# First attention of a four-stage kernel: each head's query and key rows stacked as high and low parts, 48 to a head, through a DRAM scratch

## The reference

```
def _L0_attn_ref(x, Wq, Wk, Wv, Wo):
    NH = 16
    B, T, D = x.shape
    hd = D // NH
    q = (x @ Wq.T).reshape(B, T, NH, hd).transpose(0, 2, 1, 3)
    k = (x @ Wk.T).reshape(B, T, NH, hd).transpose(0, 2, 1, 3)
    v = (x @ Wv.T).reshape(B, T, NH, hd).transpose(0, 2, 1, 3)
    att = jnp.einsum('bhtd,bhsd->bhts', q, k) / jnp.sqrt(jnp.asarray(hd, x.dtype))
    att = att + jnp.triu(jnp.full((T, T), neg, dtype=att.dtype), k=1)
    w = jax.nn.softmax(att, axis=-1)
    z = jnp.einsum('bhts,bhsd->bhtd', w, v)
    return z.transpose(0, 2, 1, 3).reshape(B, T, D) @ Wo.T
```

## Time and profile before

| | |
|---|---|
| runs | 968.06 us median (967.4, 968.06, 969.87) |
| profiled execution | 971.69 us, of which the trace spans 969.5 us |
| PE busy | 837.5 us of the span, 86% |
| DVE, ACT, POOL busy | 668.5, 389.0, 394.3 us |
| mean granted clock of TensorE | 0.916 |
| rounds 0 to 6 of the first attention | 38.74 to 239.71 us |
| round 7 and what follows it | from 239.71 us |

### The profile page before, as it was taken

The page is one execution under the profiler, slowest core; times in us unless marked ns, Lnnn a source line. Parts: engine busy times, 40 slices in busy tenths (PEclk is TensorE's granted clock), DMA queues, the critical chain, the costliest instruction groups (busy, mean ns, idle before and its releaser), DMA issues. The chain is left out here.

```text
span 969.5 us, 18748 instructions
## 1 busy us (share of the span) xinstructions
PE 837.5 (86%) x6718; PEld 702.1 (72%) x6718; DVE 668.5 (69%) x1501; ACT 389.0 (40%) x764; POOL 394.3 (41%) x548
## 2 busy tenths in 40 slices
PE   5889999998778968778898869899989999999994
PEld 4667777677557857667776758688878888788883
DVE  6657767677358644898565566577898775867876
ACT  2244444444542353333343344355556554222220
POOL 3123323333522237777776561756664221100001
PEclk9899999999889988999999976677898988999998
DMA  7002112200000057999940352211110000000001
GB/s 260 2 2 99 56 45 99 100 12 13 13 11 0 23 154 224 292 285 305 301 139 2 88 162 65 71 39 48 33 54 27 0 1 1 1 0 22 23 1 43
DMA packets 51385, 75.57 MB, mean 78 GB/s; under 512 B 9810, under 2 KB 43869, under 8 KB 51176
## 3 DMA queue, kind: packets, MB, share of 16 engines
q1 hardware_dynamic: 27624, 43.01, 13.6%
q0 software_dynamic: 9856, 18.92, 7.0%
q10 hardware_dynamic: 13824, 12.59, 3.8%
HBM read 70.27 MB, written 31.46 MB: 105 GB/s over the span
## 5 line engine op out<-in xcount | busy, mean ns | idle before, releaser
L537 POOL DMA_INDIRECT work<-xnd,rows_at x128 | 132.8, 1037 | 49.6 <-issue 42.9
L454 POOL TENSOR_SCALAR veps<-mv 128x2 f32<-128x2 f32 (+1 forms) x63 | 15.5, 246 | 284.3 <-DVE mv L1574 284.1
L463 POOL TENSOR_SCALAR_AFFINE_SELECT work<-work 128x256 f32<-128x256 f32 x128 | 53.5, 442 | 118.9 <-ACT work L659 118.8
L2013 DVE TENSOR_TENSOR work<-work,S 64x256 f32<-64x256 f32 x128 | 54.2, 424 | 55.6 <-ACT work L811 53.7
L972 PE MATMUL ZO<-parts 128*128 128x256 f32 x224 | 71.1, 318 | 16.1 <-DVE parts L1613 6.0
L972 PE MATMUL S<-xr,parts 128*128 128x512 f32 x192 | 83.0, 432 | 0.8 <-issue 0.8
L791 ACT ACTIVATE work<-S 128x512 f32<-128x512 f32 x64 | 38.2, 597 | 101.0 <-PE S L1311 97.0
L974 PE MATMUL S<-xr,parts 128*128 128x512 f32 x192 | 76.9, 401 | 0.0
L973 PE MATMUL S<-xr,parts 128*128 128x512 f32 x192 | 76.8, 400 | 0.0
L659 ACT ACTIVATE work<-S 128x768 f32<-128x768 f32 x64 | 51.7, 811 | 53.9 <-PE S L1046 53.9
L1311 PE MATMUL S<-ident,work 128*128 128x128 f32 x256 | 43.3, 293 | 28.8 <-DMA work<-xnd,rows_at 27.9
(11 more groups left out here) (331 smaller groups left out, 2337.0 us busy)
## 6 DMA issues: line engine op xcount, KB each, us to landing
yd<-work ACTq DMA_DIRECT2D x128, 128.0 KB
raw<-in_experts SPq DMA_DIRECT2D x74, 192.0 KB
work<-in_experts SPq DMA_DIRECT2D x36, 192.0 KB
lg_all<-in_experts SPq DMA_DIRECT2D x18, 192.0 KB
xnd<-attn_w SPq DMA_DIRECT2D x8, 256.0 KB, 2.1
shd<-work SPq DMA_DIRECT2D x8, 256.0 KB, 2.4
work<-xnd,rows_at POOLq DMA_INDIRECT x128
raw<-in_ffn SPq DMA_DIRECT2D x2, 1024.0 KB, 6.3
```

The lines of the kernel that those rows point to most:

```text
L463: last = pool.affine_select(out=diagonal, in_=diagonal, compare_op=ALU.is_ge, fill=0.0, base=0, pattern=[[0, 2], [1, P]], channel_multipli ...
L537: pool.indirect_dma_start(xg[:, i % RING, b, :], None, xnd[:], bass.IndirectOffsetOnAxis(ap=rows_at[:, k:k + 1], axis=0), bounds_check=NT ...
L2013: last = dve.tensor_tensor(hx[64 * half:64 * half + 64, i % 2, :], sgx[64:128, i % 2, :], S[2 + i % 2][64:128, 0:256], ALU.mult)
```

## The change

The weights are no longer doubled: a sequence has two calls of `project_qk` (c is 0 or 1) in place of four, each with the queries of eight heads and their keys. ACT writes their high parts in one copy of 512 columns (`qk_hi`), DVE their low parts in one subtraction (`qk_lo`). SP then stores high, high and low to planes of a DRAM tensor `qkd` (three transfers of 256 KB) and loads from it four blocks of 48 rows (192 KB each), in which a head's rows are query high, low, high (`QROWS`) and key high, high, low (`KROWS`), at partitions 0 to 47 for r=0 and 64 to 111 for r=1. The host orders the weights' columns for that (`units`).

One matmul over 48 rows now does what two passes did, so the turned scores are two passes: scores of 48 rows, and the selector by the row maxima, still 32 rows (`shift`). Plain scores use all 48 rows too, and unit u uses its own heads. Around it: `input_transposes` moves from u5 to u2, `project_qk(i+2, 0)` from u6 to u3, `project_qk(i+2, 1)` from u7 to u6, `router_logits` from u3 to u7; the first round (i = -1) has `project_v(0)`, `input_transposes(1)` and `project_qk(1, 0)` ahead of its units. SP stages the first three halves of sequences ahead of the later weights' loads, the fourth behind them, and the 2 MB copies to `yd` move to the last rounds. Two semaphores are merged with others.

```
-        wq_p, wk_p, wv_p, wo_p, xn_p, z_p = (in_parts(n) for n in (512, 512, D, D, T, T))
+        wq_p, wk_p, wv_p, xn_p = (in_parts(n) for n in (D, D, D, T))
+        qk_hi = parts[:, words[0]:words[0] + 2 * T]
...
+            def score_rows(b, c):
+                n = 2 * b + c
...
+                sp.wait_ge(s["a_q"], n + 1)
+                sp.dma_start(planes(0, 3), stage(qk_hi)).then_inc(s["q_st"], 16)
+                sp.dma_start(planes(2, 2), stage(qk_hi)).then_inc(s["q_st"], 16)
+                sp.wait_ge(s["a_k"], n + 1)
+                sp.dma_start(planes(1, 4), stage(qk_lo)).then_inc(s["q_st"], 16)
+                sp.wait_ge(s["q_st"], 48 * (n + 1))
+                if n:
+                    sp.wait_ge(s["q_in"], 64 * n)
+                if b >= 2:
+                    sp.wait_ge(s["a_st"], 8 * (b - 2) + 4 * c + 4)
+                for r in range(2):
+                    for first, rows in ((0, QROWS), (3, KROWS)):
+                        sp.dma_start(rows[64 * r:64 * r + 48, b % 2, 4 * c:4 * c + 4, :].bitcast(F32)
+                                     .rearrange("p u t -> p (u t)"),
+                                     qkd[c, first:first + 3, 64 * r:64 * r + 64, :]
+                                     .rearrange("k (e u) t -> k e (u t)", u=4)).then_inc(s["q_in"], 16)
...
+            for b, c in ((0, 0), (0, 1), (1, 0)):
+                score_rows(b, c)
+            later_weights()
+            score_rows(1, 1)
+            for i in range(NB + 1):
+                if i + 2 < NB:
+                    score_rows(i + 2, 0)
+                if i:
+                    normed_rows(i - 1)
+                if i + 2 < NB:
+                    score_rows(i + 2, 1)
+                if i > NB - 3:
+                    result_rows(i - NB + 2)
+            result_rows(3)
...
-            def query_copies(b, g):
-                act.wait_ge(s["a_qk"], 4 * b + g + 1)
-                act.activation(qh0, O[:, 0:T], ACT.Copy)
-                act.activation(kh0[:, b % 2, g, :], O[:, T:2 * T], ACT.Copy).then_inc(s["a_q"], 1)
+            def score_highs(b, c):
+                n = 2 * b + c
+                act.wait_ge(s["a_qk"], n + 1)
+                if n:
+                    act.wait_ge(s["q_st"], 48 * n)
+                act.activation(qk_hi, O, ACT.Copy).then_inc(s["a_q"], 1)
...
+                    if u % 4 == 0:
+                        pe.wait_ge(s["q_in"], 64 * (2 * nb + u // 4 + 1))
...
-                    for k in range(3):
+                    for shift in range(2):
                         for half in range(2):
                             for r in range(2):
-                                last = turned(r, half, k)
+                                last = turned(r, half, shift)
...
-            def key_copies(b, g):
-                dve.wait_ge(s["a_q"], 4 * b + g + 1)
-                dve.scalar_tensor_tensor(qm0[:, b % 2, g, :], qh0, negm[:, 0:1], O[:, 0:T], ALU.mult, ALU.add)
-                dve.tensor_tensor(kl0[:, b % 2, g, :], O[:, T:2 * T], kh0[:, b % 2, g, :], ALU.subtract
-                                  ).then_inc(s["a_k"], 1)
+            def score_lows(b, c):
+                dve.wait_ge(s["a_q"], 2 * b + c + 1)
+                dve.tensor_tensor(qk_lo, O, qk_hi, ALU.subtract).then_inc(s["a_k"], 1)
```

More of the change, by code:

```diff
@@ L389, in _, with planes, stage @@
[L389 to L393, removed]
+            def score_rows(b, c):
+                n = 2 * b + c
+                flat = qkd[c].rearrange("k p t -> p k t")
+                def planes(first, step):
+                    return flat[:, first:first + step + 1:step, :]
+                def stage(part):
+                    return part.bitcast(F32).rearrange("p (k t) -> p k t", k=2)
+                sp.wait_ge(s["a_q"], n + 1)
[14 more added lines that the diff above has]
+                                     .rearrange("k (e u) t -> k e (u t)", u=4)).then_inc(s["q_in"], 16)
@@ L982, in _, with project_qk @@
             M = (SS[:, 0:1024], TT)
-            def project_qk(b, g):
-                if g == 0:
+            def project_qk(b, c):
+                if c == 0:
                     pe.wait_ge(s["a_xtl"], b + 1)
                 else:
[L988 to L993, removed]
+                    pe.wait_ge(s["a_q"], 2 * b + 1)
+                    pe.wait_ge(s["a_k"], 2 * b + 1)
                 for w, o in ((wq_p, 0), (wk_p, T)):
-                    for c in range(KC):
-                        last = three(O[:, o:o + T], lambda k: w[:, k, c, g * P:(g + 1) * P],
-                                     lambda k: xn_p[:, k, c, :], c == 0, c == KC - 1)
+                    for k in range(KC):
+                        last = three(O[:, o:o + T], lambda part: w[:, part, k, c * P:(c + 1) * P],
+                                     lambda part: xn_p[:, part, k, :], k == 0, k == KC - 1)
                 last.then_inc(s["a_qk"], 1)
             def project_v(b):
-                pe.wait_ge(s["a_q"], 4 * b + 2)
-                pe.wait_ge(s["a_k"], 4 * b + 2)
+                if b >= 3:
+                    pe.wait_ge(s["a_xall"], b - 1)
+                else:
+                    pe.wait_ge(s["a_q"], 2 * b + 2)
+                    pe.wait_ge(s["a_k"], 2 * b + 2)
                 if b == 0:
                     pe.wait_ge(s["a_wl"], 3)
-                if b >= 3:
-                    pe.wait_ge(s["a_xall"], b - 1)
                 for t in range(2):
@@ L1129, in attention @@
                     maxima_rows(i)
+                if i == -1:
+                    project_v(0)
+                    input_transposes(1)
+                    project_qk(1, 0)
                 for u in range(8):
@@ L1149, in attention @@
                     if 0 <= i + 2 < NB and u == 6:
-                        project_qk(i + 2, 0)
-                if 0 <= i + 2 < NB:
-                    project_qk(i + 2, 1)
+                        project_qk(i + 2, 1)
+                    if 0 <= i - 2 < NB - 1 and u == 7:
+                        router_logits(i - 2)
             input_transposes(0)
@@ L1739, in _ @@
                 dve.wait_ge(s["a_wh"], i + 1)
-                for r in range(2):
-                    last = dve.scalar_tensor_tensor(head_pairs(wp[:, 1])[:, :, r, :], head_rows(w), scale,
-                                                    head_pairs(wp[:, 0])[:, :, r, :], ALU.mult, ALU.subtract)
-                last.then_inc(s["a_wl"], 1)
+                dve.scalar_tensor_tensor(wp[:, 1], w, scale, wp[:, 0], ALU.mult, ALU.subtract).then_inc(s["a_wl"], 1)
             def product(n):
@@ L2315, in blocks, with units @@
         return np.concatenate(gu + [d.reshape(n, P, D)], axis=2)
+    def units(w):
+        order = np.arange(D).reshape(2, 4, 2, HD0).transpose(0, 2, 3, 1).reshape(D)
+        return kmajor(w.T[:, order])
     quads = lambda w: w.reshape(D, 2, P, 4).transpose(0, 1, 3, 2).reshape(D, 1024)
```

159 lines of the change are left out of this document (82 added, 77 removed).

## The result

| | before | changed |
|---|---|---|
| median of 4 runs each, us | 968.96 (967.4 to 977.57) | 1033.49 (1026.03 to 1039.61) |
| ratio | | 1.0643 (1.0548 to 1.0738) |
| profiled execution, its span | 971.69, 969.5 | 1039.61, 1037.4 |
| first round start (L1073, now L1119) | 38.74 | 55.45 |
| rounds 0 to 6 | 200.97 | 248.36 |

The change made the kernel 6.4% slower, where I had forecast a gain of 0.7%. Of the 67.9 us in the profiled execution, 16.7 arose ahead of the first round, 47.4 in rounds 0 to 6, and 3.8 behind them. Ratios, and the medians of experiments 5 and 6, leave out runs more than 1.5% above the fastest run of the same kernel.

The account below looks back on a forecast made before the run. TensorE's list bounds a round, VectorE's chain its end. Terms: start +1.5, round 0 -3.3, stall +2.0, round 1 -0.2, middle -6.8, clock +3.3, round 6 -2.3, round 7 -0.5: -6.3, so 961.7 us, range 952 to 965 (all cases 949 to 971).

Parts of the forecast that it names:

- four loads, issued in 1.8 us and landed some 2.5 us on: Loads of a half from the DRAM scratch, within a round trip of 8.7 us in every later round.
- The cover of 13.3: Time a later round has to hide the 8.7 us trip; each us beyond costs a us in six rounds.
- the round trip is late in every round: Rival: a 17 us scratch trip costs 3.7 us in six rounds, 22 in all: 984 us, slower; chance 0.08.
- signs of being wrong: Units under 1.0 us, waits on `qkd` in the middle rounds, or clocks under 0.93 there.
- I count two more such stretches: +3.3: Stretches at 1.2 GHz behind a round's end, 1.1 to 1.65 us each; bounds -2.7 and +8.
- some 2 us: TensorE's new wait at a middle round's end, formerly hidden under unit 7's group; a round saves 1.7, not 3.1.
- 25.7 to 28.6: Start of the first scores in us, at full to half clock; first L1119 then at 40.2, +1.5.
- stall of 0.4 to 4, I take 2.0: Round 0, unit 4: us of waiting for sequence 1's fourth half, which stands behind the later weights' loads.
- A unit of 1.28 us: Plain and turned scores of a unit: 1.16 us at best, plus 0.12 for one more tile switch.
- 0.12 us taken: Cost per unit of the added switch from 48 rows to the selector's 32; bounds 0 and 0.2.
- comes back whole: Rival: all removed TensorE time, 192 projection matmuls or 25 us, is gained; about 945 us, chance 0.07.
- PE busy down by about 20 us: Sign of being right: TensorE's busy time over the execution falls by about 20 us.

Follow-up runs that it names:

- experiments 5: experiment 1's kernel with the changes of experiment 3 and experiment 4 together: selector on 48 rows, fourth half staged ahead of the later weights; 974.7 us, 1.0025.
- Experiment 6: The kernel of experiments 5 with VectorE's input statistics ahead of the low parts of the group in unit 6; 966.1 us, 0.9945.
- experiment 1: The changed kernel with the scratch loads' dimensions reordered, so that the first is 16 in place of 3; 987.05 us, 1.0202.
- experiment 10: The kernel of experiment 9 with the selector on 32 rows again, one tile switch more a unit; 950.15 us, 0.9838.
- experiment 7: The kernel of experiments 5 with the second projection group back behind unit 7, its copies after the next round's start, router logits in unit 4; 950.18 us, 0.9777.
- 9: The kernel of experiment 7 with the later weights' loads issued in round 0 and the shared experts' in round 1; 944.48 us, 0.973.
- experiment 3: The kernel of experiment 1 with the selector's matmuls on 48 rows, the tile size of the scores; 982.21 us, 1.0148.
- experiment 4: The kernel of experiment 1 with the fourth half of a sequence staged ahead of the later weights' loads; 977.75 us, 1.0113.
- experiment 2: The kernel before the change, with plain and turned scores of a unit in the same groups of 32 rows; 975.03 us, 1.0055.

## Why the prediction was wrong

**The step that failed** is "four loads, issued in 1.8 us and landed some 2.5 us on", in the start and in every later round. I took the landing from `xnd` stores of 256 KB (2.1 us) and never asked over how many engines a load with a first dimension of 3 is spread. It took 13.4 us from the first issue to release, on three engines of sixteen, and the trip 17.9 us in place of 8.7. On sixteen engines (experiment 1) the loads landed in 4.3 us, not 2.5, and were issued in 2.46, so that a trip takes some 10.6 us by my estimate: the term was too small there too, but inside the cover. The cover of 13.3 was right to 0.1, and what lay beyond it, 4.56 us in that round, became a wait, as in my "Cover gone, each us beyond 13.3 costs a us". My rival "the round trip is late in every round", with "17 us for a trip", was the case that came; it had 0.08 and 984 us. It fell short by 50 us. Half of that are the loads, worth 46 us by experiment 1 in place of my 22, since I let them act in the six later rounds alone; the other 25 us are what experiment 1 still takes beyond my 961.7. At the start, where two and then four halves stand one after the other in the queue with no cover, the waits were 10.1 us before the first round and 20.2 in round 0, more than the 22.6 of rounds 2 to 6. What stood for the rival was in the prediction ("no row shows stores and loads of such halves"); a cost bounded by no row at all deserved a wider range.

Two of my signs of being wrong came: waits on `qkd` in the middle rounds, and clocks of 0.80 to 0.90 there.

**The second wrong step is the clock**: "I count two more such stretches: +3.3", with "one in every round (+8)" as the upper bound. With the loads' waits all but gone (experiment 1), 67.9 us of rounds 0 to 6 ran at 1.2 GHz against 10.2 before. What the term should have been shows beside experiment 10, where the same work in the same tiles, in another order, ran at 0.98 (first experiment 1, then 10):

```profile
43.14:253.60 210.46, 193.36 (x2015) 145.67 (x2015) 126.89 (x309) 78.70 (x130) 60.16 (x146) 0.84 0.47 124
```

```profile
41.07:218.57 177.50, 167.47 (x2016) 128.29 (x2015) 130.19 (x309) 77.28 (x130) 60.98 (x144) 0.98 0.57 149
```

That is 26 us of busy time for the +3.3, though not all of it need reach the end. I had found the wait at L1119 and priced it well ("some 2 us": 11.7 in 8 times, up to 2.7), but took it to cost little besides. Before, VectorE's chain kept TensorE for less at the same place, by the waits from 30 to 260 us:

```profile
PE ZO L1073 <- DVE work L1634: 3.5, 7, 1.0
```

Experiment 6 shows what it does cost besides, and experiment 7 that it needn't exist: the group that stood in unit 7 was the cover of that chain. My text said so ("What was hidden under the group of unit 7 is now a wait of some 2 us"), and let it eat into a round's gain (1.7 us in place of 3.1), but hardly into the clock. Why the clock falls in one round's end and not in another's I can't settle; the runs show only that it went with waits of 1 to 3 us, and that in rounds 2 to 5 of experiments 7 and 9 it was gone with them.

**Start and fourth half.** The first scores started at 30.12, later than my 25.7 to 28.6, and with the loads repaired the first L1119 is at 43.14, where I took 40.2 and had 41.0 as a bound. The "stall of 0.4 to 4, I take 2.0" of the fourth half was 1.7 in experiment 1, but only because TensorE came late at 1.2 GHz; it was 5.53 in experiment 3, beyond my bound. Setting it right won 9 us (experiment 4), of round 0's 8.1 us 4.9 by the late half and at most 3.2 by the clock.

**Right.** A unit of 1.28 us was 1.29 to 1.31; three passes in a row group one after another, beside those of other row groups (experiment 2); the switch to the selector's 32 rows, 0.12 us taken, 0.14 to 0.16 measured (experiments 10 and 3), so that units alone give nothing back. "Rounds of about 28 us" holds for the quicker ones of experiments 1 and 3 (27.8 to 28.8, at a clock of 0.94), and the projection groups' 3.1 us a round are real: with the chain covered and the switch gone a round falls by 4.9 us, from 29.7 to 24.8, and TensorE's busy time in it by 3.4 (27.05 to 23.64). I had put the rival that this time "comes back whole" at 945 us and 0.07; it needed another order and other loads, and then came to 944.48. "PE busy down by about 20 us" holds there, against the earlier trace rows:

```profile
PE 816.0 (86%) x6270; PEld 679.1 (72%) x6270; DVE 654.5 (69%) x1453; ACT 375.9 (40%) x716; POOL 395.3 (42%) x548
```

## What to carry to other kernels

Before a transfer is costed by its bytes, look at the first dimension of its pattern and at the DMA share of a stretch in which it runs alone: 0.19 there is three engines of sixteen, and reordering the pattern was worth 46 to 89 us. Before a block of TensorE work is moved away from a round's end, ask which chain it covers; the wait that appears costs itself and, in the traces of experiments 5 and 6, several times itself in granted clock. A short wait is no proof that a transfer is nearly in time: the engine may only have come late, as in round 0 of experiment 1. When a round trip joins a queue, count every transfer ahead of and behind it, most of all at the start, where nothing covers it.

## What the runs showed of the hardware

A transfer that uses three engines also holds up those behind it on its queue: `xnd` landed 11.1 us after its issue behind such loads, 4.4 behind loads of sixteen, and 2.1 with no loads there. And with one chain shorter by 0.94 us a round five rounds took 16.4 us less, 12.8 of it busy time, at a mean clock of 0.93 in place of 0.83 for the same 1519 matmuls. Matmuls of one row group ran one after another (plain and turned scores 0.28 us apart), and a change from 64-row to 32-row tiles in a unit cost 0.14 us.
